# Low parts moved from GpSimd to VectorE in attention, and fp32 projections in the mixture

## What is computed

```
h = conv_tower(x)
h = h + attention(layernorm(h))        # 32 heads, 8 groups of keys and values, 128 positions
h = h + mixture(layernorm(h))          # 8 experts of rank 16, the best one taken
h = h + correlation_of_delays(layernorm(h))
h = h + dense_layer_plus_experts(layernorm(h))

# the mixture:
logits = x @ route_w.T;  v, i = top_1(logits)
out = (one_hot(i) * v * (x @ A.T)) @ B       # x @ A.T has 8 * 16 = 128 columns
```

## Time and profile before

| | us |
|---|---|
| runs | 3115.19, 3120.15, 3120.9 (median 3120.15) |
| the profiled execution | 3115.31, of which the span of the profile is 3113.6 |
| convolution and first rows | to about 311 |
| attention | about 311 to 2512.3 |
| mixture | 2512.3 to 2636.4 |
| delays, dense layer | 2636.4 to 3113.6 |

### The profile page before, as it was taken

How to read it: one execution, slowest core, us unless ns; L and a number is a source line. 1 busy time by engine, 2 the same in 40 slices (tenths; PEclk the granted TensorE clock), 3 DMA queues, 4 the chain that set the end, 5 groups by cost and what they waited for, 6 DMA issues and landing times. The chain is left out here.

```text
span 3113.6 us, 37983 instructions
## 1 busy us (share of the span) xinstructions
PE 2854.7 (92%) x13353; PEld 2308.7 (74%) x13353; DVE 1594.4 (51%) x2914; ACT 982.6 (32%) x2029; POOL 915.5 (29%) x394
## 2 busy tenths in 40 slices
PE   8993999999899999989999998999999878749999
PEld 6762777777777777777777777777777667538888
DVE  4886544455544445555444455544445457563222
ACT  3553323333332223333222333232233223531111
POOL 2110433344333334433333442333334100241010
PEclk9995999999999999999999999999999978879999
DMA  5320322223222222322222232222223111010000
GB/s 114 69 54 9 102 75 74 74 88 93 63 75 75 74 74 88 91 65 76 75 74 74 81 93 63 82 75 74 74 71 91 34 55 41 1 61 28 28 27 28
DMA packets 55613, 207.20 MB, mean 67 GB/s; under 512 B 6928, under 2 KB 7312, under 8 KB 53456
## 3 DMA queue, kind: packets, MB, share of 16 engines
q1 hardware_dynamic: 55504, 205.79, 22.2%
HBM read 197.37 MB, written 8.39 MB: 66 GB/s over the span
## 5 line engine op out<-in xcount | busy, mean ns | idle before, releaser
L728 POOL TENSOR_TENSOR at_wlo<-at_wstage,at_whi 128x1024 fp32r<-128x1024 f32 x192 | 477.7, 2488 | 1437.0 <-ACT at_whi L751 1437.0
L993 PE MATMUL at_proj<-qr_xhi,at_whi 128*128 128x512 f32 x1536 | 635.1, 413 | 53.4 <-POOL at_wlo L728 49.0
L995 PE MATMUL at_proj<-qr_xhi,at_wlo 128*128 128x512 f32 x1536 | 609.3, 397 | 0.0
L994 PE MATMUL at_proj<-qr_xlo,at_whi 128*128 128x512 f32 x1536 | 608.8, 396 | 0.0
L993 PEld LDWEIGHTS at_proj<-qr_xhi,at_whi 128*128 128x128 f32 x1536 | 290.2, 189 | 131.2 <-issue 52.7
L994 PEld LDWEIGHTS at_proj<-qr_xlo,at_whi 128*128 128x128 f32 x1536 | 290.3, 189 | 69.9 <-issue 7.5
L995 PEld LDWEIGHTS at_proj<-qr_xhi,at_wlo 128*128 128x128 f32 x1536 | 289.5, 188 | 70.5
L1041 PE MATMUL at_out<-at_wohi,at_ohi 128*128 128x512 f32 x1008 | 314.3, 393 | 8.2 <-DVE at_wolo L720 6.2
L720 POOL TENSOR_TENSOR at_wolo<-at_ostage,at_wohi 128x1024 fp32r<-128x1024 f32 x126 | 312.0, 2497 | 32.7 <-ACT at_wohi L757 32.7
L1041 PE MATMUL at_out<-at_wolo,at_ohi 128*128 128x512 f32 x1008 | 312.5, 391 | 0.0
L1041 PE MATMUL at_out<-at_wohi,at_olo 128*128 128x512 f32 x1008 | 312.5, 391 | 0.0
(11 more groups left out here) (253 smaller groups left out, 4537.1 us busy)
## 6 DMA issues: line engine op xcount, KB each, us to landing
at_wstage<-in_w_qkv_dram SPq DMA_DIRECT2D x192, 512.0 KB, 3.6
at_ostage<-in_w_o_dram SPq DMA_DIRECT2D x128, 512.0 KB, 3.8
cv_x<-in_x_dram SPq DMA_DIRECT2D x32, 512.0 KB, 6.6
out_dram<-h SPq DMA_DIRECT2D x16, 512.0 KB, 2.7
fn_w_lo_raw<-in_w_t_dram SPq DMA_DIRECT2D x8, 512.0 KB, 6.6
fn_qka_lo_raw<-in_qka_t_dram SPq DMA_DIRECT2D x5, 512.0 KB, 5.4
sc_fhi_raw<-in_dft_fwd_dram SPq DMA_DIRECT2D x4, 512.0 KB, 7.1
sc_chi_raw<-in_lag_cos_dram SPq DMA_DIRECT2D x2, 512.0 KB, 9.5
```

Of the source, the lines that this page charges most:

```text
L728: pool.tensor_tensor(w_lo[j % 2][:, :], w_stage.buffers[j % 2][:, :], w_hi[j % 2][:, :].bitcast(F32), ALU.subtract).then_inc(wlo_done, 1)
L993: pe.matmul(proj[:, j % 2, :], hi[:, w], x_hi[:, k, :], start=(k == 0), stop=False)
L994: pe.matmul(proj[:, j % 2, :], hi[:, w], x_lo[:, k, :], start=False, stop=False)
L995: last = pe.matmul(proj[:, j % 2, :], lo[:, w], x_hi[:, k, :], start=False, stop=(k == KT - 1))
```

## The change

In attention every low part is made by DVE: POOL has no instructions left in that stage. DVE's list takes the subtractions `low_w` and `low_o` between its own work, and ACT rounds w2 earlier, ahead of `pT_out` and the second `soft` (in other steps ahead of o2). SP waits for the same events in the same order.

In the mixture the projections and the output product become one plain fp32 matmul each instead of three fp32r ones. The weights are used as loaded, the transposed rows are copied by ACT into an fp32 tile (`copy`), and the transposed `wh` likewise, into two buffers; DVE's subtractions go. PE's order in a pass becomes: projections of tile t, transposes of tile t + 1, output product of tile t - 1, transpose of `wh`. PE waits for the A weights ahead of its first projection and for B ahead of its first output product. The rest of the program, the convolution too, has no edit.

The diff, cut to what does this (constructors and names of semaphores are left out):

```diff
@@ -704,41 +703,10 @@
-                            if nxt:
+                            if ahead == 0 or nxt:
-                            elif what[1] == 0:
-                                after(sp, wolo_done, s * HEADS + 1)
-                            elif what[1] == 1:
-                                sp.wait_ge(wolo_dve, 1)
-                            if ahead == 0 or nxt:
-
-            def low_o(e, s, r, done):
-
-                after(e, wohi_done, s * HEADS + r + 1)
-                e.tensor_tensor(wo_lo[:, r, :], o_stage[r % 2][:, :], wo_hi[:, r, :].bitcast(F32), ALU.subtract)\
-                 .then_inc(done, 1)
-
-            @block.gpsimd
-            def _(pool):
-
-                def split_w(n, j):
-                    after(pool, whi_done, n + 1)
-                    pool.tensor_tensor(w_lo[j % 2][:, :], w_stage.buffers[j % 2][:, :], w_hi[j % 2][:, :].bitcast(F32),
-                                       ALU.subtract).then_inc(wlo_done, 1)
-
-                def first():
-                    split_w(0, 0)
-
-                def step(qt, g, par, att, nxt, turn):
-                    s = head_at(qt, g)
-                    for what in splits(att, nxt):
-                        if what[0] == "w":
-                            split_w(tile_at(s + what[1], what[2]), what[2])
-                        elif nxt or what[1] % 2 == 0:
-                            low_o(pool, s, what[1], wolo_done)
-                steps(pool, first, step)
...
@@ -813,14 +781,15 @@
                         pT_out(n + 1)
                         rows.high(act, qt + 1, proj, 3)
                         split(("w", 1, 1), ("o", 0), ("o", 1))
+                        split(("w", 1, 2))
                     elif att:
                         soft(n, 0)
-                        split(("w", 1, 1), ("o", 0), ("o", 1))
+                        split(("w", 1, 1), ("o", 0), ("o", 1), ("w", 1, 2))
                         pT_out(n)
                         soft(n + 1, 1)
                     else:
-                        split(("w", 1, 1))
-                    split(("w", 1, 2), ("o", 2))
+                        split(("w", 1, 1), ("w", 1, 2))
+                    split(("o", 2),)
                     if nxt:
                         v_out(s + 1)
                     if att:
...
@@ -893,6 +862,16 @@
+                def low_w(s, j):
+                    after(dve, whi_done, tile_at(s, j) + 1)
+                    dve.tensor_tensor(w_lo[j % 2][:, :], w_stage.buffers[j % 2][:, :], w_hi[j % 2][:, :].bitcast(F32),
+                                      ALU.subtract).then_inc(wlo_done, 1)
+
+                def low_o(s, r):
+                    after(dve, wohi_done, s * HEADS + r + 1)
+                    dve.tensor_tensor(wo_lo[:, r, :], o_stage[r % 2][:, :], wo_hi[:, r, :].bitcast(F32),
+                                      ALU.subtract).then_inc(wolo_done, 1)
+
...
@@ -923,25 +902,34 @@
                         top_of(n, 0)
                         normalize(n)
                     if nxt:
+                        low_w(s + 1, 1)
+                    if att:
+                        low_o(s, 0)
+                        low_o(s, 1)
+                    if nxt:
                         rope_out(s + 1, 1 - par, 0)
+                    if att and not turn:
+                        top_of(n + 1, 1)
+                    if nxt:
+                        low_w(s + 1, 2)
                     if att:
                         if not turn:
-                            top_of(n + 1, 1)
-                            if not nxt:
-                                low_o(dve, s, 1, wolo_dve)
                             normalize(n + 1)
                         top_of(n + 2, 2)
                         o_split(n)
+                        low_o(s, 2)
+                        low_o(s, 3)
                         normalize(n + 2)
                     if nxt:
+                        low_w(s + 1, 3)
                         rope_out(s + 1, 1 - par, 2)
                     if att:
-                        if not nxt:
-                            low_o(dve, s, 3, wolo_dve)
                         top_of(n + 3, 3)
                         o_split(n + 1)
                         add(qt, n, 0, nxt)
                         normalize(n + 3)
+                    if nxt:
+                        low_w(s + 1, 4)
                     if stats:
                         rows.stats(dve, stats_of, link, 0)
                     if nxt:
...
@@ -951,6 +939,8 @@
+                    if nxt:
+                        low_w(s + 1, 5)
@@ -960,6 +950,8 @@
+                    if nxt > 1:
+                        low_w(s + 2, 0)
@@ -973,7 +965,7 @@
-                steps(dve, lambda: None, step)
+                steps(dve, lambda: low_w(0, 0), step)
...
@@ -1028,11 +1020,8 @@
-                    if b == 0 and nxt:
+                    if b == 0:
-                    elif b == 0:
-                        after(pe, wolo_done, s * HEADS + HEADS // 2)
-                        pe.wait_ge(wolo_dve, HEADS // 2)
...
@@ -1211,6 +1203,22 @@
+
+    def turn(self, pe, t):
+
+        after(pe, self.normed, t + 1)
+        after(pe, self.hi_done, t)
+        for k in range(KT):
+            last = pe.transpose(self.tp[:, k // 4, (k % 4) * P:(k % 4 + 1) * P],
+                                self.xn[:, k * P:(k + 1) * P], self.ident[:, :])
+        last.then_inc(self.turned, 1)
+
+    def copy(self, act, t, par, used, count):
+
+        after(act, self.turned, t + 1)
+        after(act, used, count)
+        act.copy(self.x[par][:, :, :], self.tp[:, :, :].rearrange("p a (k t) -> p (a k) t", t=P))\
+           .then_inc(self.hi_done, 1)
...
@@ -1367,28 +1375,24 @@
-                    ar.high(act)
-                    rows.high(act, 0, 0, pj_done, 0)
+                    rows.copy(act, 0, 0, pj_done, 0)
-                    b.high(act)
-                        rows.high(act, t + 1, (i + 1) % 2, pj_done, t)
+                        rows.copy(act, t + 1, (i + 1) % 2, pj_done, t)
-                    after(act, out_mm, t)
-                    act.copy(wt_hi[:, :], wt[:, 0:P]).then_inc(wthi_done, 1)
+                    if not early(t, 2):
+                        after(act, out_mm, t - 1)
+                    act.copy(wt_sb[i % 2][:, :], wt[:, 0:P]).then_inc(wt_done, 1)
-                    ar.low(dve)
-                    rows.low(dve, 0, 0)
-                    b.low(dve)
...
@@ -1416,14 +1420,9 @@
-                    if on(1):
-                        rows.low(dve, t + 1, (i + 1) % 2)
-                    after(dve, wthi_done, t + 1)
-                    dve.tensor_tensor(wt_lo[:, :], wt[:, 0:P], wt_hi[:, :].bitcast(F32), ALU.subtract)\
-                       .then_inc(wtlo_done, 1)
...
@@ -1436,38 +1435,33 @@
-                    ar.ready(pe)
-                    b.ready(pe)
-
-                def outputs(t):
-                    after(pe, wtlo_done, t + 1)
+                    pe.wait_ge(ar_in, 16)
+
+                def outputs(t, par):
+                    after(pe, wt_done, t + 1)
-                        w = slice(c * BANK, (c + 1) * BANK)
-                        pe.matmul(out[:, c, :], wt_hi[:, :], b.hi[:, w], start=True, stop=False)
-                        pe.matmul(out[:, c, :], wt_hi[:, :], b.lo[:, w], start=False, stop=False)
-                        mm = pe.matmul(out[:, c, :], wt_lo[:, :], b.hi[:, w], start=False, stop=True)
+                        mm = pe.matmul(out[:, c, :], wt_sb[par][:, :], b[:, c * BANK:(c + 1) * BANK],
+                                       start=True, stop=True)
-                    after(pe, rows.lo_done, t + 1)
+                    after(pe, rows.hi_done, t + 1)
+                    after(pe, wh_done, t)
+                    for k in range(KT):
+                        mm = pe.matmul(pj[:, 0:ROUTED], rows.x[i % 2][:, k, :], ar[:, k * ROUTED:(k + 1) * ROUTED],
+                                       start=(k == 0), stop=(k == KT - 1))
+                    mm.then_inc(pj_done, 1)
-
-                    after(pe, wh_done, t)
-                    xh, xl = rows.x_hi[i % 2], rows.x_lo[i % 2]
-                    for k in range(KT):
-                        w = slice(k * ROUTED, (k + 1) * ROUTED)
-                        pe.matmul(pj[:, 0:ROUTED], xh[:, k, :], ar.hi[:, w], start=(k == 0), stop=False)
-                        pe.matmul(pj[:, 0:ROUTED], xh[:, k, :], ar.lo[:, w], start=False, stop=False)
-                        mm = pe.matmul(pj[:, 0:ROUTED], xl[:, k, :], ar.hi[:, w], start=False, stop=(k == KT - 1))
-                    mm.then_inc(pj_done, 1)
-                        outputs(t - 1)
+                        if early(t, 2):
+                            pe.wait_ge(b_in, 16)
+                        outputs(t - 1, (i + 1) % 2)
-                    after(pe, wtlo_done, t)
+                    after(pe, wt_done, t)
-                tile_steps(pe, before, body, lambda: outputs(NB - 1))
```

(24 more changed lines are left out.)

5 lines of the change are left out of this document (2 added, 3 removed).

## The result

The changed kernel takes 3032.49 us (median of 4 runs, 3032.19 to 3032.67) against 3119.72 (4 runs, 3115.19 to 3120.9): a ratio of 0.9723, 95% interval 0.9706 to 0.974. The forecast was 3043 us, in a range from 3026 to 3075. The profiled execution took 3032.52 us, its span 3030.8, 82.8 less than before.

A forecast was written before the change was run, and what follows sets the result against it. Attention was taken to be bound by TensorE, busy 2046 of 2116 us. Attention -42, last step -1 and mixture -31 make -74 against 3115.3: 3041.3; with half of 4.8 on top 3043 us, range 3026 to 3075.

The forecast's parts named there:

- Attention, the stop: In 28 attention steps projection 2's 1.48 us wait for GpSimd's low part of w2 goes: -42 us, bounds -33 and -50.
- The margins: In an attention step, data ready before TensorE asks: second probabilities 0.5 us, batch 0's output product 1.2, w2 2.3.
- Rival (a): Attention's stop stays in another place, each step waiting 1 to 1.5 us again: 3079 us, chance 0.10.
- The last step: Attention's last step, where TensorE waits 6.2 us for the low parts of o: -1 us, bounds -2 and +2.
- The mixture: The whole mixture stage, by an earlier start, shorter passes and less half clock: -31 us, bounds -36 and -12.
- The start: Mixture: first projection at 2519.2 instead of 2528.82, between 2518.4 and 2522.7, waiting for the later of data and transposed rows: -9.6 us.
- The pass: Mixture: a pass takes 4.55 us instead of 5.41, saving 0.86 us, 13 us over 15 passes.
- The clock: Mixture: plain passes bring full clock back at about 2524 instead of 2545, 8 us back; 2 us more behind the coefficients.
- Rival (b): The mixture stays at half clock, a pass taking 8.9 us: +25 instead of -31, 3099 us, chance 0.09.
- Rival (c): In attention a VectorE subtraction costs 3.06 us, not 1.21: +263 against -74, about 3300 us, chance 0.03.
- Behind the stage: After the mixture nothing is edited: 0, bounds -3 and +3 us for where the clock falls.
- The 2 us on top: Added to the whole time: half of the 4.8 us by which the runs' median lay above the profiled execution.

The follow-up runs named there:

- e4b: The kernel before with VectorE making all of attention's low parts, but ScalarE still rounding w2 behind the second softmax: 3098.8 us, ratio 0.9943.
- e7b: The changed kernel with four more VectorE statistics over 128x512 in each attention step, behind the subtractions for the first two output weights: 3084.16 us, ratio 0.9898.
- e3b: The kernel before with only ScalarE's order edited, w2 rounded right behind o1; GpSimd still makes the low parts: 3067.98 us, ratio 0.9847.
- e1b: The kernel before with the attention part of the change alone: 3064.94 us, ratio 0.9837.
- e5b: The changed kernel with the mixture's transposes of tile t+1 put ahead of the projections of tile t again: 3038.3 us, ratio 0.9743.
- e8b: The changed kernel with VectorE's last four statistics and the coefficients moved ahead of the mixture's first pass: 3028.73 us, ratio 0.9717.
- e6b: The changed kernel with the mixture's projections as three fp32r products again, in the new order of groups: 3064.78 us, ratio 0.9838.
- e2b: The kernel before with the mixture part of the change alone: 3085.86 us, ratio 0.9901.

## Why the prediction was right, point by point

**Attention, the stop.** It was found where it was and went, and next to nothing came in its place (0.4 us behind VectorE's low part, 1.7 more behind probabilities). The mis-sized term is the price of one stop: "28 x 1.48" should have been 28 x 1.74 = 48.7. The idle time shown ahead of a matmul counts from the end of the last one, but matmuls overlap, so that without a stop the next one starts earlier than that end: in the step shown of the changed kernel the transposes end at 1028.26 + 0.60 = 1028.86, and the projection behind them starts at 1028.62. The surplus is the same in three places: 1.74 against 1.48, 1.14 against 0.92 (e4b), 1.45 against 1.23 (e7b): 0.22 to 0.26 us for each stop. The distance of starts gives it directly: in the earlier trace rows projection 2 starts 2.97 us behind the scores, and after 1.25. The bound of -50 still held the stop; with the last step, attention came to -52.2, just outside the two terms' bounds.

**Why it went.** I laid it on both edits together. e3b and e4b part them: the order gives 48.9 us alone, the engine 18.1 alone, both 52.0. The other 3 us of the move to VectorE lie within the noise of the totals (0.9831 to 0.9864 and 0.982 to 0.9853). The traces show more: attention ends 5.6 us sooner in e1b than in e3b (2462.16 and 2467.74), and the mixture, which neither edits, happens to take 2.8 us more there, at half clock for 16.6 us instead of 10.4. The 318 subtractions put 386 us on VectorE's list, but its busy time in attention grew by only 210 (1275.32 instead of 1065.40), as its own work no longer stood still beside GpSimd.

**The margins.** Forecast 0.5, 1.2 and 2.3 us for the second probabilities, batch 0's output product and w2; the trace of after shows 1.05, 1.35 (1034.31 less 1032.96) and 2.7. The first was larger because the rope and the maximum took 3.48 us (1021.09 to 1024.57) without GpSimd, where I had kept the 3.8 with it. Rival (a), the stop in another place, did not come. It is real all the same: e7b has it, at 1.45 us a step, with 2.39 us more on VectorE's list, and e4b has it where one of the two edits is left out.

**The last step: -1 forecast, -3.7 measured** (53.66 us from its first maximum to its last add, then 49.92). The row of TensorE at its first output product, beside the earlier trace rows:

```profile
2425.59 1.19 PE L1030 MATMUL at_out<-at_wohi,at_ohi 128*128 128x512 f32 x2 [4.25 <-DVE at_wolo L872]
```

The wait is 4.25 instead of 6.2, and the product starts 1.6 us sooner after the first maximum, which is within the term's bounds. Another 1.6 is the clock: between VectorE's last but two and last but one adds it was 9.66 us before (2496.64 to 2506.30) and 8.07 after (2445.78 to 2453.85). TensorE was at half clock there for 3 us before (1.00, 0.68, 0.50, 0.50, 0.62, 1.00 in the windows of 1 us from 2496 to 2502) and at full clock after. In e1b, whose attention is the same as after, it was 9.68, and in e3b and e4b, which keep one half of the old attention each, 8.09 and 8.07. So this part is luck and not the change's, and the forecast had no term for it.

**The mixture: -31 forecast, -32.0 measured.** The start: -9.6 forecast, -9.6 measured; the later of data and transposed rows was right (the row waits for ScalarE's copy of them), but 2519.2 was a choice in a range of 4.3 us without a working, so that it came out to the tenth is luck. The pass: 4.55 and 4.55, priced from one plain pass of 128 columns and from the 0.86 us of two at 512 (projections 1.85 for 1.81, output product 1.72 for 1.72, transposes 0.88 for 0.79, the transpose of `wh` 0.11 for 0.2: the two misses cancel). By the Trainium skill, page "FP8 and Floating Point Precision", section "TensorE Precision Notes" (four passes for true fp32), with one pass for an fp32r product, the projections should have become dearer. They became cheaper: 16 plain instructions from 2536.57 to 2538.42 are 1.85 us, and 24 fp32r ones took 2.72. What failed is not the count for plain products, whose cost goes with the columns (0.86 x 136 / 512 = 0.23 us, measured 1.85 / 8 = 0.23), but my reading that an fp32r product is one pass: at 136 columns it took 0.113 us, half of a plain one. The clock: full at 3.1 us after the first projection, forecast at about 5; the half clock behind the coefficients was to cost 1.7 us, and it cost 1.7 (2493.77 to 2500.00 is 6.23 us, less 4.56). Rival (b) was the wrong way round: with plain passes the half clock is the shorter one, and the table shows it with either order. Laid out, the stage's end should read 2605.2 and not 2605.4, which changes nothing.

**Rival (c)**, a VectorE subtraction of 3.06 us: 1.22 us measured, with GpSimd idle. The four slow ones in the dense layer ran from 2774.65 to 2786.64, all beside work of GpSimd, and in the changed kernel they are as slow (12.0 us for four). No run took GpSimd away from them, but e3b shows the effect on other instructions, 1.65 us for a negation and 1.09 for probabilities beside GpSimd, 0.17 and 0.69 without it, and the negation ends where GpSimd's subtraction does. This agrees with the Trainium skill, page "SBUF — State Buffer", section "Who interferes with whom".

**Behind the stage**: +1.7, within the ±3. In e5b and e8b, with the same code there, the same stretch took 477.5 us, near the 477.2 of before.

**The 2 us on top.** I had added them because the runs before spread over 5.7 us, with the median 4.8 above the profiled one. The changed kernel's four runs lie within 0.5 us and its profiled one at the median: this term had no cause in the trace, and it wasn't there.

## What to carry to other kernels

Ask of a stop which queue order makes the data late before moving work to another engine: one moved entry in ScalarE's list brought 48.9 of 52.0 us, the other engine without it 18.1. Price a stop by the distance of starts with and without it, not by the idle time shown. And when a stage sits at half clock while it is busy, look at the kind of its matmuls: here a plain fp32 product of 136 columns was cheaper than three fp32r ones at full clock (0.23 us against 0.34), and the half clock was shorter besides (3.4 us or none against 10.2 behind the same standstill).

## What the runs showed of the hardware

The granted clock fell while TensorE was busy: in e6b it came back at 2471.9, stayed at 1.00 through a standstill of 1.95 us and for the first 1.4 us of fp32r products of 136 columns that followed (from 2473.91), and was 0.50 from 2476 to 2482 though TensorE never paused. Standing still did not always lower it: in e2b, whose passes are plain, TensorE stood still for some 3 us behind the coefficients and the clock stayed at 1.00, where in the changed kernel, with the same passes, the same standstill was followed by half clock. With fp32r products of 136 columns the half clock behind that standstill lasted 10.2 us in each of five runs, though TensorE was busy nearly throughout. An fp32r product took 0.113 us at 136 columns and 0.23 at 512 (the starts of projections in the step above are 0.23 apart), so a narrow one does not cost in proportion: 136 columns would be 0.06.

A VectorE instruction that meets a GpSimd subtraction ends with it: four negations of 128x4, in the kernel before and in e3b, end 0.02 to 0.03 us behind a subtraction (1042.71 and 1042.68; 1047.63 and 1047.60; 1029.40 and 1029.37; 1034.55 and 1034.53), and they last as long as that takes, 1.05 to 1.65 us instead of 0.17. A multiplication of 128x512 for the probabilities ends 0.54 to 0.55 us behind one (1052.87 and 1052.32 before; 1032.27 and 1031.73, 1038.07 and 1037.53 in e3b), 1.09 to 2.69 us instead of 0.69.
